# Graph-network kernel on one Trainium2 core: when GpSimd waits for the row gathers of a slot, and when it announces the slot

## What is computed

```python
xn = layernorm(x)
x  = x + gnn(xn, src, dst) + mix(xn)      # three attention layers over the edges; one linear-attention block
x  = x + ffn(layernorm(x))                # router, 8 experts of 256 -> 512 -> 256, two of them kept for each node

# one gnn layer
h  = x @ W                                # 8 heads of 32
e  = leaky_relu(el[src] + er[dst], 0.2)
a  = exp(e - m[dst]) / segment_sum(exp(e - m[dst]), dst)
out[n] = sum over the edges with dst == n of h[src] * a
```

## Time and profile before

| what | value |
|---|---|
| median of three runs | 7180.35 us |
| span of the profiled execution | 9455.6 us |
| TensorE busy | 6144.4 us (65%) |
| VectorE busy | 4611.0 us (49%) |
| GpSimd busy | 4509.0 us (48%) |
| ScalarE busy | 1586.2 us (17%) |
| row gathers in the records (line 423) | 4716, that is 1179 slots of four, 393 to a layer |

### The profile page before, as it was taken

How to read it: one execution, slowest core, us unless ns; L and a number is a source line. 1 busy time by engine, 2 the same in 40 slices (tenths; PEclk the granted TensorE clock), 3 DMA queues, 4 the chain that set the end, 5 groups by cost and what they waited for, 6 DMA issues and landing times.

```text
span 9455.6 us, 145971 instructions
## 1 busy us (share of the span) xinstructions
PE 6144.4 (65%) x35030; PEld 4782.0 (51%) x35031; DVE 4611.0 (49%) x11211; ACT 1586.2 (17%) x4669; POOL 4509.0 (48%) x4739
## 2 busy tenths in 40 slices
PE   4555656666666455555555555555677788889999
PEld 3344444444444333434444444333556677777888
DVE  5444444444454444444444444445555555555554
ACT  2000000000001000000000000000123334444555
POOL 2555555445444555555554444465544444443332
PEclk8666777777777767767777777767889999999999
DMA  5333333333333333333333333333333322222221
GB/s 195 107 107 105 107 102 101 95 101 104 100 101 96 98 106 107 101 99 101 98 97 97 92 90 92 83 113 111 99 95 92 95 85 82 77 77 75 74 71 45
DMA packets 386097, 916.19 MB, mean 97 GB/s; under 512 B 130561, under 2 KB 192777, under 8 KB 385930
## 3 DMA queue, kind: packets, MB, share of 16 engines
q0 software_dynamic: 227904, 681.63, 26.3%
q1 hardware_dynamic: 115530, 194.09, 6.4%
q10 hardware_dynamic: 42624, 40.02, 1.3%
HBM read 871.89 MB, written 43.49 MB: 97 GB/s over the span
## 4 chain that ended last, share of the span: by engine, by line
PE 36%; another core or an unknown queue 22%; issue 18%; DVE 11%; DVEq 10%; ACT 2%; ACTq 1%; DMA 1%; POOL 0%; SPq 0%; POOLq 0%
PE bank L1465 22%; PE bank L1390 6%; PE bank L1379 5%; DVEq L255 3%; DVE sel L1141 3%; DVE selT L1102 2%; DVE lg L1121 1%; PE bank L1433 1%; DVEq L1141 1%; DVEq L1121 1%; ACT region L513 1%; DVE msg L1131 1%; ACT L513 1%; DVEq L1201 1%
## 5 line engine op out<-in xcount | busy, mean ns | idle before, releaser
L423 POOL DMA_INDIRECT gat<-table,meta x4716 | 4495.6, 953 | 4797.2 <-DVE sel L1141 1596.8
L1465 PE MATMUL bank<-msg,sel 128*128 x10560 | 3714.7, 506 | 1943.1 <-DVE sel L1141 1164.0
L1465 PEld LDWEIGHTS bank<-msg,sel 128*128 128x128 f32 x10560 | 2454.3, 247 | 2589.1 <-issue 2132.6
L1131 DVE SCALAR_TENSOR_TENSOR msg<-bank,gat 128x1056 f32 x1320 | 1657.9, 1256 | 355.1 <-ACT bank L556 213.9
L1141 DVE TENSOR_TENSOR sel<-iota_t,meta 128x256 f32<-128x256 f32 x2640 | 1043.3, 421 | 1337.6 <-remote 823.6
L556 ACT ACTIVATE bank<-lg 128x32 f32<-128x32 f32 x1320 | 263.1, 199 | 6417.1 <-DVE lg L1125 5385.2
L1433 PE MATMUL bank<-uvb,selT 128*128 (+1 forms) x10584 | 432.2, 173 | 969.2 <-DVE selT L1102 718.4
L1433 PEld LDWEIGHTS bank<-uvb,selT 128*128 128x128 bf16 x10584 | 408.3, 101 | 1263.1 <-DVE selT L1102 707.4
L1121 DVE TENSOR_TENSOR lg<-gat,bank 128x64 f32<-128x64 f32 x880 | 193.8, 220 | 1407.1 <-remote 1097.1
L1379 PE MATMUL bank<-xT,w 128*128 128x128 f32 x6272 | 796.3, 282 | 55.5 <-issue 55.3
L1390 PE MATMUL bank<-w,region 128*128 128x256 f32 x3136 | 787.2, 394 | 65.7 <-ACT region L513 31.6
(11 more groups left out here) (215 smaller groups left out, 2618.0 us busy)
## 6 DMA issues: line engine op xcount, KB each, us to landing
dstb<-dst_lists SPq DMA_DIRECT2D x297, 512.0 KB
gat<-table,meta POOLq DMA_INDIRECT x4716
table<-hrow ACTq DMA_DIRECT2D x98, 140.0 KB
w<-in_W SPq DMA_DIRECT2D x2, 4096.0 KB
table<-hrow SPq DMA_DIRECT2D x49, 140.0 KB, 1.7
region<-xnT_d ACTq DMA_DIRECT2D x50, 128.0 KB
region<-qT_d ACTq DMA_DIRECT2D x50, 128.0 KB
res<-in_x SPq DMA_DIRECT2D x1, 6272.0 KB, 25.3
```

The lines of the kernel that those rows point to most:

```text
L423: pool.indirect_dma_start(gat[:, r, c, :], None, table[l], bass.IndirectOffsetOnAxis(meta[:, m, c, 0:1].bitcast(U32), 0)).then_inc(s_done, 16)
L1131: dve_v.scalar_tensor_tensor(msg[:, bass.ds(n % 2, 1), :, :].rearrange("p a c (h d) -> p (a c) h d", h=H), ex_p.unsqueeze(3).to_broadcast( ...
L1465: last = pe.matmul(acc[:, 0:MSG], sel[:, c, :], msg[:, bass.ds(m % 2, 1), c, :].rearrange("p a m -> p (a m)"), start=opens and c == 0, sto ...
```

## The change

GpSimd issues the four gathers of a slot, waits until all four have landed, announces the slot, and only then goes on to the next slot's waits and gathers. The number of gathers, waits and announcements is the same; the wait for a slot's landing moves from behind the third gather of the next slot to directly behind its own fourth gather.

```diff
                 for c in range(CH):
                     gather_row(1, 1, c, slot_in[l][1])
+                announce(1, 1)
                 with pool.Fori(0, rounds) as i:
                     for j in range(LISTS):
-                        m, before, r = (j + 2) % LISTS, (j + 1) % RING, (j + 2) % RING
+                        m, r = (j + 2) % LISTS, (j + 2) % RING
                         if m % BATCH == 0:
                             pool.wait_ge(list_ready[l], LISTS * i + j + 2)
                             pool.sem_inc(turn_taken, 1)
@@
                         pool.sem_inc(turn_taken, 1)
                         for c in range(CH):
                             gather_row(m, r, c, slot_in[l][r])
-                            if c + 2 == CH:
-                                announce(before, 2 * i + j // RING + 1)
-                announce(1, 2 * rounds + 1)
+                        announce(r, 2 * i + (j + 1) // RING + 1)
```

## The result

The changed kernel took 9926.99 us (median; 9924.98 to 9928.31), the kernel before 7178.33 us beside it: the ratio is 1.383, 95% interval [1.381, 1.385]. The forecast was 9330 us with a range of 8600 to 9750 us. The direction came out as forecast, and so did the main mechanism, a GpSimd loop that now waits for each landing in turn; the time was 597 us above the forecast and 177 us above the end of the range.

What follows compares the result with a forecast made beforehand. It took the kernel to be GpSimd-bound in layers 1 and 2 and mostly TensorE-bound in layer 3. At 7.45 us a slot instead of 5.00: 328 + 5856 + 3144 = 9328 us, range 8600 to 9750.

Steps and rivals of the forecast that it cites:

- The plain sum for before: Kernel before: 328 us around the loops, 3930 for layers 1 and 2 at GpSimd's pace, 2676 for layer 3: 6934 us.
- (a): GpSimd's pace in plain runs is somewhat quicker than the trace's: period 6.7 us, 8565 us; chance 0.12.
- (b): The trace stretches GpSimd's pace in full: 5.7 us a slot after the change, 7180 to 7300 us; chance 0.02.
- (c): Consumers are as slow in plain runs as in the trace, so only early tiles pay: 7450 us; chance 0.03.
- (d): VectorE's and TensorE's uneven times add, some 5 us a tile in layers 1 and 2: 9830 us; chance 0.06.
- (e): Announcement goes out earlier, by up to three gathers (3.75 us), which helps a waiting VectorE: 7150 us; chance 0.02.
- Step 1: GpSimd's four gathers of a slot, from the first one's start to the last one's end: 4.70 us.
- Steps 2 and 4: Landing behind the last gather's end, 1.49 us, plus 0.10 us a slot for SyncE's list loads (bound 0.6).
- Step 3: GpSimd from landing through announcement and buffer wait to the next gather: 0.81 us, plus 0.35 for the second wait.
- The sum: GpSimd's period for a slot: 4.70 + 1.49 + 0.81 + 0.35 + 0.10 = 7.45 us, bounds 6.9 to 8.4.
- the prediction's own rule: Whole kernel: 328 us around the loops, 2 x 393 periods for layers 1 and 2, plus layer 3: 9328 us.
- Layer 3: Each tile of s slots costs the larger of 7.45 s and 32.3 + 2.03 (s + 1): 3144 us, 468 more.

Runs made afterwards that it cites:

- before_again: The kernel before, unchanged, run again for a trace beside its own plain time: 7190 us, profiled span 7193.2 us.
- three_gathers_b: The kernel before with three row gathers a slot instead of four (fourth group zeros), second run: 6654 us, 0.926 of a kernel before of 7191 us.
- wait_after_1_b: The kernel before with landing wait and announcement behind the next slot's first gather, second run: 8328 us, 1.159 of 7191 us (first run, wait_after_1: 8364, 0.894 of 9353).
- after_small_lists: The changed kernel with SyncE's destination lists loaded to 16 partitions instead of 128: 9608 us, 1.338 of a kernel before of 7182 us.
- after_three_gathers: The changed kernel with three gathers a slot instead of four (fourth group zeros): 8592 us, 0.919 of a kernel before of 9341 us.
- wait_after_4: The kernel before with landing wait and announcement moved behind the next slot's fourth gather: 9359 us, 1.001 of a kernel before of 9353 us.
- before_small_lists: The kernel before with SyncE's destination lists loaded to 16 partitions instead of 128: 9363 us, 1.001 of a kernel before of 9341 us.
- sync_announces: The kernel before with landing waits and announcements moved from GpSimd to SyncE, between its list loads: 7189 us, 1.001 of a kernel before of 7182 us.
- after_third: The changed kernel as it is, run a third time: 9962 us, 1.066 of a kernel before of 9341 us.

## Where the prediction was right, and which step failed

**The bound.** Right. The plain sum for before, GpSimd at 5.0 us a slot in layers 1 and 2, is what before_again shows (5.23 and 5.18), and three_gathers_b moved it. That the trace's extra 2275 us lie in the consumers was right as well: the 9350-chips have them. Rivals (a) and (b), by which taking records stretches GpSimd's pace, fall: records stretch nothing (7193 beside 7190 us, 9926 beside 9927), and a gather lasts as long in either condition (0.946 us in the median of the first trace, 0.949 in before_again). Rival (c), consumers as slow as in the trace, is what the 9350-chips have: the change costs 1.066 there, and (c) had reckoned 7450 us, 4% more, for it. Rival (d), 9830 us, is nearest to the measured time by luck: it put some 5 us on each of 98 tile boundaries of layers 1 and 2, and there VectorE's releases ended 6 us of GpSimd's idle time in all (2 waits; the other 337 us of the 343 lie in layer 3). Rival (e) had a premise that doesn't hold: today's announcement isn't up to three gathers late, but goes out 0.38 us behind the landing (before_again), so there was nothing to gain.

**Step 1, four gathers.** 4.70 us was one undisturbed slot; the mean of layers 1 and 2 is 4.80. Some gathers take up to 1.75 us. 0.10 us.

**Steps 2 and 4, the landing.** An undisturbed one is 1.54 us behind the gather's end (forecast 1.49). The mean is 1.89, since every fourth slot has 2.8 us. The prediction had the cause, and a bound of 0.6 us a slot, and took 0.10 "since it meets a slot's last gather only part of the time". That is the step that failed, and the largest part of the miss. 20% of the loads of before_again are issued near a slot's last gather (22% in the first trace), but 223 of 297, 75%, in the changed kernel. The landing is 3.05 us behind the gather there and 1.57 us elsewhere. The likely reason is lockstep: SyncE waits for a release by VectorE, VectorE for the announcement, and the announcement now for the landing, so the load comes at the same place of its slot again and again. Which place that is depends on the kernel: in wait_after_1_b, a chain of the same kind, 224 of 297 loads stand near a slot's first gather and 37 near its last. 1.89 against 1.59 us: 0.30 us, confirmed by after_small_lists. The bound had its own error: its 2.4 us for one meeting came from a single row and was 1.5 us in the mean.

**Step 3, the restart.** From the landing to the announcement's record it is 0.38 us, from there to the next gather's start 0.92 us undisturbed and 0.98 in the mean; 1.36 against 1.16 us. It was the first term that was too low, not the second. wait_after_1_b passes one wait between landing and gather, and takes 0.38 + 0.76 = 1.14 us undisturbed, where the prediction took 0.81 from a release by VectorE; a landing with its announcement isn't such a release. The second wait adds 0.92 - 0.76 = 0.16 us; 0.35 had been put down. In the mean 0.20 us too little.

**The sum.** 4.80 + 1.89 + 0.38 + 0.98 = 8.05 us against 7.45. By layers, from first gather to first gather: 3187 against 2957, 3180 against 2959, and the third with the tail 3379 against 3232 us. Together 598 us. With 8.05 us in place of 7.45 the prediction's own rule gives 328 + 2 x 393 x 8.05 + 3300 = 9955 us, 0.3% above the measured time: the period is the whole miss. The forecast's own period bound of 8.4 held 8.05, and 10,329 us for it stood in the text; the range was cut at 9750 for a case called unlikely.

**Layer 3.** That TensorE's expert work covers part of it was right: late tiles take 773 us in the changed kernel, in before_again and in wait_after_1_b alike. So was the rule, the larger of two sums in each tile: with a period of 8.05 us it gives 3300 us for layer 3, and from its first gather to its last the trace has 3293.

**What the profile was to show.** Gaps of 2.5 to 3.0 us in front of a slot: 2.84 to 2.89 undisturbed, 3.25 in the mean of layers 1 and 2. VectorE waiting for the announcement (866 waits of `lg`, 3926 us, against 42) and the releases' idle time shrinking to hundreds: as said. The profiled span grew by 470 us, within the 270 to some 740 that the text gave, and the plain time by 2749: also as said, since the trace of before had the slow consumers and the runs of before hadn't. The Trainium skill's 2.0 us plus bytes over 436 GB/s ("DMA: Bandwidth & Descriptors", "Anatomy of one DMA — SWDGE (gpsimd) path") gives 2.33 us from issue; this trace has 0.95 + 1.54 = 2.49 undisturbed. The Trainium skill's remark in the same section that generating descriptors costs little is not borne out for gathers of 128 rows: one gather less takes 1.27 us of GpSimd's time off a slot by the traces, and 1370 us off the plain runs of after_three_gathers, 1.16 us for each of the 1179 gathers left out.

## What to carry to other kernels

A wait for a DMA belongs far enough behind its issue that other issues cover landing and restart, here 3.7 us with three gathers against the 2.7 us (1.54 + 0.38 + 0.76) that they take undisturbed: the price of moving it up was 60, 1080 and 1600 us for the gathers given away one after another, and none of it shows in the engine's busy time. The wait stops the sequencer, not what it has issued, so standing three gathers back delayed the announcement of before_again by nothing in the median. When a wait turns loops of several engines into one chain, what ran beside them at changing places can settle at one: the share of meetings in the trace of before (22%) doesn't carry over, and the place has to be worked out, or the disturbance priced at nearly every meeting. And set the time of the profiled execution against the plain runs before reading idle times: where they differ by a third, the trace may be of another condition of the chip, and the durations of single instructions carry over where the waits don't.

## What the runs showed of the hardware

The kernel before takes 7180 us on some chips and 9350 on others, each time within 0.4% of the median over 13 runs, at a mean granted TensorE clock of 0.90 and 0.80. The waits that differ are those for TensorE's results. Two lines of the first trace (9456 us); before_again has none of the kind ("remote" means that the records name no releaser):

```profile
DVE lg L1121 <- remote: 1097.1, 229, 17.9
DVE sel L1141 <- remote: 823.6, 371, 6.7
```

Worked out from the records (each `sel` half needs the sum of the same half of the visit before): in the first trace 424 of these came over 1 us after both VectorE was free and the matmul that releases them had ended in the records, 1075 us in all; in wait_after_4 and before_small_lists, on the 9350-chips, 358 and 393; in before_again, sync_announces and after_third none, in wait_after_1 on the same chip as the slow kernel before 4. One of them in the first trace: the four matmuls end at 272.2, VectorE is idle, and `sel` starts at 275.60.

```profile
271.08 1.14 PE L1465 MATMUL bank<-msg,sel 128*128 x4
...
275.60 0.42 DVE L1141 TENSOR_TENSOR sel<-iota_t,meta 128x256 f32<-128x256 f32 x1 [5.30 <-remote]
```

85% of the 424 follow matmuls that ended while the granted clock was at 2.4 GHz, against 22% of the waits for TensorE that weren't late. So they go with the clock's upper level, and mostly come soon after it is granted (half of them within 2.0 us, half of the others at that level within 5.9 us). The kernels whose GpSimd needs 6.4 us a slot or more (wait_after_1, after_third, after_three_gathers) hardly have them on the same chips. Whether the chip holds back TensorE, whose ends are modelled in the records, or its semaphores is open, and so is why only some chips do it; no experiment told these apart. The two conditions mean that wait_after_1, 16% slower than the kernel before on one chip, is 11% faster on another.
